# The last two units of attention values behind the next queries' transposes and scores

## Chip, core and metric

The kernel runs on one core of a Trainium2 chip. The metric is the device time of one execution in microseconds (us), as the median of several runs. The core has five engines with a queue each: TensorE (PE; its weight loads are shown as PEld), VectorE (DVE), ScalarE (ACT), GpSimd (POOL) and SyncE (SP). Each takes its instructions in the order of its queue, and the engines wait for one another by semaphores.

## What is computed

Two transformer blocks on x of shape (16, 256, 128) in float32. Each block is a layer norm and a mixture of experts (half weight), an attention, and a second mixture of experts. The first block's attention is causal with rotation and decay; the second one's has normed heads and no mask. Cut to what the change touches:

```python
# block 0, causal
scores = einsum('bhqd,bhkd->bhqk', q_rot, k_rot) / sqrt(8) + decay_bias   # 16 heads of 8
attn = softmax(where(causal, scores, -inf))
out = einsum('bhqk,bhkd->bhqd', attn, v)
x = x + reshape(out) @ Wo.T
# block 1, no mask
q, k, v = (layernorm_per_head(x @ W + b) for W, b in (...))
probs = softmax(einsum('bqhd,bkhd->bhqk', q, k) * 8 ** -0.5)
x = x + reshape(einsum('bhqk,bkhd->bqhd', probs, v)) @ Wo + bo
```

## The kernel before

The program is a row of stages: routing, experts, causal attention (`a0`), experts, routing, experts, second attention (`a1`), experts, and the last sum. Both attentions are one function, `attention_stage`, with a flag `causal`. It handles one batch of 256 tokens per step and keeps several batches in flight: in step s, TensorE makes the scores of batch s, the exponents' arguments and the values of batch s-1, the output of batch s-2, the routing of batch s-3, and the operands and projections of batches s+1 and s+2. `looped_steps` runs steps -3 to 18, the middle ones in a loop.

The order on each engine is written out by hand in its own `step`. A batch's attention is cut into 16 units of two heads and one half of the queries or keys. For a unit, TensorE makes raw scores (L1494) in one of two banks psS, VectorE takes their row maxima (L1066), and the maxima of all units, written into the query operand by `max_rows` (L1072, L1073), go through TensorE again: `queries` (L1513) transposes the query operand with its maxima, half t=0 into bank psA and half t=1 into psD. VectorE copies the first half to QM (L1080, `queries_out`), ScalarE the second (L1345). Then `e` (L1531, opened in the causal stage by a mask product, L1523) makes scores minus maxima, ScalarE takes the exponent into one of four buffers PT (L1362), and `unit_v` (L1555) multiplies by the values: two matmuls of 32 rows per unit into psV, for the units 8 to 15 into psV[1].

At the end of a step TensorE transposes the last operand (`operands`, L1473, n=3), does the values of units 14 and 15, and the next step begins with the queries of the batch whose maxima are done, the first two units' scores, the transposes of the routed rows (`routed_tiles`, L386) and the first exponent argument. The second half of the queries may not start before ScalarE has copied the operand n=2 out of psD (L1338, the copy a_KT<-a_psD).

VectorE closes a step with a row of jobs: `last_operand_out` (L1087), `queries_out` (L1080), `weighted_out` (L1093, which copies psV[1] of batch s-1 and waits for all 16 units of its values), `norm.dve_apply` of batch s+3 (L317, a_attn_out), `route.dve_norm` of batch s-2 (L314 and L317, a_route_out). The next step begins with the first unit's maximum (L1066). TensorE's routed transposes wait for a_route_out; its third unit of scores waits for the first unit's maximum; `back` (L1568) waits for `weighted_out`.

POOL has the scatter of routed rows, the reciprocal roots, in the causal stage the rotation, and in the second stage the scaling of heads (`scale_heads`, L961, L965, L969). The lines around the place are these:

```python
                if has(s + 1):
                    operands(s + 1, v, 3)
                if has(s - 1):
                    unit_v(s - 1, v, UNITS - 2)
                    unit_v(s - 1, v, UNITS - 1)
```

Of the kernel before, what the change touches and what calls it, by code (L numbers as in the profile page):

```python
# [662 lines left out]
def has(b, count=BATCHES):  # L663

    return not isinstance(b, int) or 0 <= b < count
# [113 lines left out]
def attention_stage(nc, keep, tag, slots_in, slots_out, causal, params, router, router_bias, capacity):  # L779
# [17 lines left out]
    with ExitStack() as ctx:  # L797
# [10 lines left out]
        UNITS = 16  # L808
# [98 lines left out]
        def unit_b(c):  # L907

            return c // 8, (c % 8) // 2, c % 2
# [509 lines left out]
        def _(pe):  # L1419
# [70 lines left out]
            def scores(u, c, hh):  # L1490
                t, g, r = unit_b(c)
                cols = P if causal and t == 0 else SEQ
                k = 2 * g + hh
                ins = nc.tensor.matmul(  # L1494
                    psS[c % 2][:, hh, 0:cols], QT[u][64 * r:64 * r + MAXR, k, t * P:(t + 1) * P],
                    KT[u][64 * r:64 * r + MAXR, k, 0:cols], start=not causal, stop=True, skip_group_check=True)
                if hh == 1:
                    ins.then_inc(s_S, 1)

            def queries(b, u, t):  # L1500
                if t == 0:
                    pe.wait_ge(s_m, b + 1)

                if has(b + 1):
                    pe.wait_ge(s_QK[1 + t], b + 2)
                elif t == 0:
                    pe.wait_ge(route.s_xnT, b - 2)
                else:
                    pe.wait_ge(route.norm.s_var, b - 1)
                src = ext[u][:, t, 0, :, :].rearrange("p h r -> p (h r)")  # L1510
                dst = (psA, psD)[t][:, :].bitcast(BF16)
                for k in range(8):
                    last = nc.tensor.transpose(dst[:, k * P:(k + 1) * P], src[:, k * P:(k + 1) * P], identb[:, :])  # L1513
                last.then_inc(s_Xm, 1)
# [91 lines left out]
            def step(s, u):  # L1606
                v = 1 - u
                if has(s - 1):
                    queries(s - 1, v, 0)
                    queries(s - 1, v, 1)  # L1610
                if has(s):
                    for c in range(2):
                        scores_open(s, c)
                    for hh in range(2):
                        for c in range(2):
                            scores(u, c, hh)
                if has(s - 3):
                    routed_tiles(s - 3, v)
                if has(s - 1):
                    e_open(s - 1, 0)  # L1620
                    for hh in range(2):
                        e(v, 0, hh)
                for n in range(UNITS):

                    if has(s) and n < UNITS - 2:
                        scores_open(s, n + 2)
                    if has(s - 1) and n < UNITS - 1:
                        e_open(s - 1, n + 1)
                    for hh in range(2):
                        if has(s) and n < UNITS - 2:  # L1630
                            scores(u, n + 2, hh)
                        if has(s - 1) and n < UNITS - 1:
                            e(v, n + 1, hh)

                    if has(s - 1) and n >= 2 and n % 2 == 0:
                        unit_v(s - 1, v, n - 2)
                        unit_v(s - 1, v, n - 1)
                    if n == 0 and has(s - 2):
                        back(s - 2, u, 0)
                    if n == 2 and has(s + 2):  # L1640
                        tiles(s + 2, u)
                    if n == 3 and has(s - 3):
                        logits(s - 3, v)
                    if n == 4 and has(s - 2):
                        back(s - 2, u, 1)
                    if n == 4 and has(s + 2):
                        project(s + 2, 0)
                    if n == 6 and has(s - 3):
                        route.pe_P(pe, s - 3, v, psD)
                    if n == 7 and has(s - 2):  # L1650
                        divided(s - 2)
                    if n == 7 and has(s + 2):
                        project(s + 2, 1)
                    if n == 10 and has(s - 2):
                        output(s - 2)
                    if n == 12 and has(s + 1):
                        operands(s + 1, v, 0)
                    if n == 13 and has(s + 1):
                        operands(s + 1, v, 1)
                    if n == 14 and has(s + 1):  # L1660
                        operands(s + 1, v, 2)
                if has(s + 1):
                    operands(s + 1, v, 3)
                if has(s - 1):
                    unit_v(s - 1, v, UNITS - 2)
                    unit_v(s - 1, v, UNITS - 1)

            looped_steps(pe, -3, 4, 12, 18, step)


# [381 lines left out]
```

## Time and profile before

| what | us |
|---|---|
| median of 3 runs | 1972.28 |
| lowest, highest | 1964.04, 1979.4 |
| profiled execution | 1987.22 |
| its span | 1985.4 |
| TensorE, VectorE, POOL, ScalarE busy | 1354.7, 1180.1, 938.6, 718.6 |

The profile is one execution; its times are counted from the start of its span. The causal attention runs from about 330 to 735, the second one from about 1240 to 1780. In a table of stretches, PEclk is the share of TensorE's full clock that was granted. In a row of the timeline the brackets name the idle time ahead of the first instruction and what ended it.

### The profile page before, as it was taken

What the parts mean: (1) busy time and instruction counts of PE and PEld (TensorE: products, weight loads), DVE (VectorE), ACT (ScalarE), POOL (GpSimd) and SP (SyncE); (2) the same over time, 40 slices, a digit from 0 to 9 for tenths busy, and PEclk for the clock granted to TensorE, in tenths of its full rate; (3) what the DMA queues carried; (4) which work ended last, traced back from release to release, by engine and by line L of the source; (5) the groups of instructions that cost most, each with busy time, mean ns of one, the idle gap of its engine ahead of it and who ended that gap; (6) DMA issues with size and microseconds to landing.
All of it is one profiled execution on the core that took longest, in us unless ns stands there. A gap on an engine that the chain in (4) does not pass through costs nothing. (4 is left out here: it accounts for less than half of the span.)

```text
span 1985.4 us, 34923 instructions
## 1 busy us (share of the span) xinstructions
PE 1354.7 (68%) x10592; PEld 870.5 (44%) x10592; DVE 1180.1 (59%) x4230; ACT 718.6 (36%) x1339; POOL 938.6 (47%) x1276
## 2 busy tenths in 40 slices
PE   1319955988889973992329944776777777856980
PEld 1208952444444433992218841333333333325870
DVE  3632226788887651225855536888777787743555
ACT  1102222766665531220003412554444545522330
POOL 2844543345444321554755745445454554333670
PEclk9999985999998896995559975786676677767995
DMA  6152220000000005222237840000000000015864
GB/s 227 45 116 61 73 64 16 12 23 26 22 16 12 12 17 115 72 69 76 72 81 213 245 137 16 11 12 12 16 16 16 16 6 12 8 33 159 236 199 130
DMA packets 93868, 134.91 MB, mean 68 GB/s; under 512 B 14784, under 2 KB 72512, under 8 KB 93760
## 3 DMA queue, kind: packets, MB, share of 16 engines
q1 hardware_dynamic: 62768, 88.27, 16.3%
q0 software_dynamic: 17408, 35.82, 5.3%
q10 hardware_dynamic: 13584, 9.48, 2.0%
q8 instruction: 56, 0.92, 0.2%
q14 instruction: 52, 0.43, 0.1%
HBM read 80.61 MB, written 52.91 MB: 67 GB/s over the span
## 5 line engine op out<-in xcount | busy, mean ns | idle before, releaser
L1362 ACT ACTIVATE a_PT<-a_psE 128x512 f32<-128x512 f32 (+1 forms) x512 | 275.5, 545 | 296.1 <-PE a_psE L1531 292.0
L1066 DVE TENSOR_REDUCE a_mx<-a_psS 128x2 f32<-128x512 f32 (+1 forms) x512 | 309.3, 617 | 22.6 <-PE a_psS L1494 21.9
L1494 PE MATMUL a_psS<-a_KT,a_QT 54*128 54x256 bf16 (+1 forms) x1024 | 206.0, 304 | 81.8 <-DVE a_mx L1066 69.4
L1531 PE MATMUL a_psE<-a_QM,a_KT 56*128 56x256 bf16 (+1 forms) x1024 | 209.0, 304 | 1.9 <-issue 0.8
L1555 PE MATMUL a_psV<-a_PT,a_vx 128*32 128x256 f32 (+1 forms) x2048 | 183.3, 436 | 0.0
L1946 POOL DMA_INDIRECT slots_y<-e_y,e_ids x160 | 155.3, 970 | 46.6 <-issue 24.4
L1876 PE MATMUL e_psH<-e_rowsT,e_w 128*128 128x256 f32 x640 | 162.6, 399 | 9.0 <-DMA e_w<-in_pack 7.6
L1494 PEld LDWEIGHTS a_psS<-a_KT,a_QT 54*128 54x128 bf16 x1024 | 60.7, 100 | 217.8 <-issue 119.0
L1793 POOL DMA_INDIRECT slots_y<-e_y,e_ids x128 | 124.2, 971 | 48.7 <-POOL e_ids L1791 29.2
L1876 PEld LDWEIGHTS e_psH<-e_rowsT,e_w 128*128 128x128 f32 x640 | 119.7, 197 | 28.1 <-issue 7.0
L1765 ACT ACTIVATE e_hT<-e_psH 128x1024 f32<-128x1024 f32 x64 | 65.5, 1023 | 183.0 <-PE e_psH L1738 183.0
L1738 PE MATMUL e_psH<-e_rowsT,kept_w 128*128 128x256 f32 x512 | 126.5, 392 | 2.1 <-DVE e_rowsT L1774 2.1
L1906 ACT ACTIVATE e_sg<-e_psH,e_w 128x256 f32<-128x256 f32 x160 | 67.1, 470 | 167.6 <-PE e_psH L1876 167.6
L1747 PE MATMUL e_psY<-kept_w,e_hT 128*128 128x128 f32 x1024 | 124.9, 276 | 0.0
L1747 PEld LDWEIGHTS e_psY<-kept_w,e_hT 128*128 128x128 f32 x1024 | 119.9, 193 | 0.1
L1774 DVE COPY e_rowsT<-e_psT 128x256 f32<-128x256 f32 x64 | 27.2, 425 | 146.9 <-PE e_psT L1730 146.9
L1915 DVE COPY e_rowsT<-e_psT 128x256 f32<-128x256 f32 x80 | 34.0, 425 | 129.7 <-PE e_psT L1869 129.7
L1738 PEld LDWEIGHTS e_psH<-e_rowsT,kept_w 128*128 128x128 f32 x512 | 95.7, 197 | 14.4 <-DVE e_rowsT L1774 3.5
L986 POOL TENSOR_TENSOR a_left<-a_left,a_ext 128x512 f32<-128x512 f32 x32 | 37.0, 1157 | 134.9 <-DVE a_ext L1055 134.9
L982 POOL TENSOR_TENSOR a_left<-a_qk,a_ext 128x512 f32<-128x512 f32 x32 | 37.0, 1157 | 112.0 <-DVE a_ext L1051 112.0
L522 POOL TENSOR_TENSOR a_rows<-a_rows,no_rows 128x4 int32<-128x4 int32 x32 | 6.3, 198 | 170.2 <-DVE a_rows L514 170.2
L1443 PE MATMUL a_psA<-a_wqkv,a_xaT 128*128 128x384 f32 x128 | 76.2, 688 | 15.3 <-DVE a_pr L1027 9.1
(328 smaller groups left out, 3189.1 us busy)
## 6 DMA issues: line engine op xcount, KB each, us to landing
e_w<-in_pack SPq DMA_DIRECT2D x80, 450.0 KB, 4.0
e_rows<-slots_x SPq DMA_DIRECT2D x80, 129.0 KB, 3.0
e_rows<-spans_x SPq DMA_DIRECT2D x64, 129.0 KB, 2.1
a_got<-slots_y SPq DMA_DIRECT2D x32, 256.0 KB
t_got<-slots_y SPq DMA_DIRECT2D x32, 256.0 KB, 2.9
slots_y<-e_y,e_ids POOLq DMA_INDIRECT x288, 2.2
spans_x<-tail ACTq DMA_DIRECT2D x8, 516.0 KB, 13.6
spans_x<-tail SPq DMA_DIRECT2D x8, 516.0 KB, 17.3
```

Of the source, the lines that this page charges most:

```text
L1066: nc.vector.tensor_reduce(mx[u][:, t, 4 * g + r:4 * g + r + 3:2], psS[c % 2][:, :, 0:cols], AX, ALU.max).then_inc(s_max, 1)
L1362: nc.scalar.activation(PT[:, c % 4, :, q0:SEQ], psE[c % 2][:, :, q0:SEQ], ACT.Exp).then_inc(s_e, 1)
L1443: nc.tensor.matmul(psA[:, 0:QKV], xaT[:, t * P:(t + 1) * P], wqkv[:, :], start=True, stop=True).then_inc(s_proj, 1)
L1494: ins = nc.tensor.matmul(psS[c % 2][:, hh, 0:cols], QT[u][64 * r:64 * r + MAXR, k, t * P:(t + 1) * P], KT[u][64 * r:64 * r + MAXR, k, 0:co ...
L1531: ins = nc.tensor.matmul(psE[c % 2][:, hh, q0:SEQ], KT[u][64 * r:64 * r + MAXR + 2, k, kt * P:(kt + 1) * P], QM[64 * r:64 * r + MAXR + 2, ...
L1555: last = nc.tensor.matmul(psV[g // 2][32 * quad:32 * quad + 32, g % 2, q0:SEQ], vx[u][:, kt, head, :], PT[:, c % 4, hh, q0:SEQ], start=(kt ...
L1738: last = nc.tensor.matmul(psH[j % 2][:, c, :], w[:, j // KEPT_TILES, c * P:(c + 1) * P], rowsT[:, j % 2, :], start=True, stop=True)
L1747: last = nc.tensor.matmul(psY[j % 2][:, s * D:(s + 1) * D], hT[:, j % 2, c, s * P:(s + 1) * P], w[:, j // KEPT_TILES, UP + c * D:UP + (c + ...
L1793: pool.indirect_dma_start(slots_out, bass.IndirectOffsetOnAxis(ap=ids[:, j % U, s:s + 1].bitcast(U32), axis=0), y[:, j % U, s, :], None).t ...
L1876: last = nc.tensor.matmul(psH[u % 2][:, c, :], w[:, u, c * P:(c + 1) * P], rowsT[:, u % 2, :], start=True, stop=True)
L1906: ins = nc.scalar.activation(sg[:, u % 2, c, :], psH[u % 2][:, c, :], ACT.Silu, bias=w[:, u, B1 + c:B1 + c + 1])
L1946: pool.indirect_dma_start(slots_out, bass.IndirectOffsetOnAxis(ap=ids[:, u, s:s + 1].bitcast(U32), axis=0), y[:, u, s, :], None).then_inc( ...
```

## The change

The values of units 14 and 15 leave the end of the step. In the next step they stand behind the queries (both halves) and the scores of the first two units, and ahead of the routed transposes. The batch is then numbered s-2, and its buffers have the index u.

```diff
@@ -1614,6 +1614,9 @@
                     for hh in range(2):
                         for c in range(2):
                             scores(u, c, hh)
+                if has(s - 2):
+                    unit_v(s - 2, u, UNITS - 2)
+                    unit_v(s - 2, u, UNITS - 1)
                 if has(s - 3):
                     routed_tiles(s - 3, v)
                 if has(s - 1):
@@ -1661,9 +1664,6 @@
                         operands(s + 1, v, 2)
                 if has(s + 1):
                     operands(s + 1, v, 3)
-                if has(s - 1):
-                    unit_v(s - 1, v, UNITS - 2)
-                    unit_v(s - 1, v, UNITS - 1)
 
             looped_steps(pe, -3, 4, 12, 18, step)
```

On TensorE, at a step's boundary in the causal stage (`a_psV<-a_PT` are the values, `a_psA` and `a_psD<-a_identb` the two halves of the queries, `a_psS` the masks and scores):

```order
 L1473 MATMUL a_psD<-a_identb,a_ext 128x128 x8
 L1473 MATMUL a_psV<-a_identb,a_ext 128x128 x8
-L1555 MATMUL a_psV<-a_PT,a_vx 32x128 x4
 L1513 MATMUL a_psA<-a_identb,a_ext 128x128 x8
 L1513 MATMUL a_psD<-a_identb,a_ext 128x128 x8
 L1486 MATMUL a_psS<-a_masks,a_identb 128x2x128 x2
 L1494 MATMUL a_psS<-a_KT,a_QT 128x128 x4
+L1555 MATMUL a_psV<-a_PT,a_vx 32x128 x4
 L386 MATMUL a_psA<-ident,a_route_out 128x128 x2
 L1523 MATMUL a_psE<-a_masks,a_identb 128x2x128
```

Four matmuls pass 16 transposes, two masks and four score products; nothing else changes place.

The same place in the second attention stage, where the values have 256 columns and there are no masks:

```order
 L1473 MATMUL a_psD<-a_identb,a_ext 128x128 x8
 L1473 MATMUL a_psV<-a_identb,a_ext 128x128 x8
-L1555 MATMUL a_psV<-a_PT,a_vx 32x256 x4
 L1513 MATMUL a_psA<-a_identb,a_ext 128x128 x8
 L1513 MATMUL a_psD<-a_identb,a_ext 128x128 x8
 L1494 MATMUL a_psS<-a_KT,a_QT 128x256 x4
+L1555 MATMUL a_psV<-a_PT,a_vx 32x256 x4
 L386 MATMUL a_psA<-ident,a_route_out 128x128 x2
 L1531 MATMUL a_psE<-a_QM,a_KT 128x256 x2
```

Here too the values stand ahead of the routed transposes and the first exponent argument.

VectorE's queue is the same in both kernels. Its row from the copy of the weighted values (L1093) over the loop's end to the first maximum of the next step (L1066):

```order
L1093 COPY a_oT<-a_psV 128x512
L169 REGISTER_ALU
L317 TENSOR_SCALAR a_attn_out<-x_res,a_attn_mv,a_attn_rstd 128x128 x2
L314 ISA
L314 COPY a_route_out<-ids 128x4
L317 TENSOR_SCALAR a_route_out<-x_res,a_route_mv,a_route_rstd 128x2x128 x2
L194 ISA
L652 REGISTER_ALU
L652 COMPARE_AND_BRANCH
L1066 TENSOR_REDUCE a_mx<-a_psS 128x2
```

Nothing moved in it; its first row waits for the matmuls that moved on TensorE.

## Rows read from the trace of the kernel before

**Rows 1.** The page, its first part: busy time, share and instructions.

```profile
PE 1354.7 (68%) x10592; PEld 870.5 (44%) x10592; DVE 1180.1 (59%) x4230; ACT 718.6 (36%) x1339; POOL 938.6 (47%) x1276
```

**Rows 2.** Stretches: length, busy PE, PEld, DVE, ACT, POOL; PEclk; DMA share; GB/s.

```profile
391.33:581.88 190.55, 170.34 (x1916) 89.22 (x1914) 162.91 (x569) 125.62 (x264) 95.58 (x119) 1.00 0.07 23
581.88:691.58 109.70, 100.20 (x954) 48.62 (x952) 75.28 (x260) 62.49 (x129) 44.15 (x54) 0.81 0.03 11
1339.98:1691.61 351.63, 259.27 (x2074) 120.12 (x2075) 269.21 (x759) 170.86 (x320) 174.00 (x253) 0.71 0.04 13
...
611.90:625.50 13.60, 13.60 (x80) 6.03 (x82) 6.95 (x32) 6.36 (x16) 2.31 (x2) 0.50 0.01 1
```

**Rows 3.** Timeline of TensorE: start, length, engine, line, operation, count, idle before.

```profile
607.58 0.42 PE L1555 MATMUL a_psV<-a_PT,a_vx 128*32 128x128 f32 x8
607.93 0.62 PE L1513 MATMUL a_psA<-a_identb,a_ext 128*128 128x128 bf16 x8
608.39 0.61 PE L1513 MATMUL a_psD<-a_identb,a_ext 128*128 128x128 bf16 x8
608.84 0.38 PE L1486 MATMUL a_psS<-a_masks,a_identb 128*128 128x256 bf16 x2
609.15 0.28 PE L1494 MATMUL a_psS<-a_KT,a_QT 54*128 54x128 bf16 x4
611.25 0.41 PE L386 MATMUL a_psA<-ident,a_route_out 128*128 128x128 f32 x2 [1.82 <-DVE a_route_out L317]
```

**Rows 4.** Timeline of ScalarE, the same boundary.

```profile
607.31 1.01 ACT L1338 COPY a_KT<-a_psD 128x1024 bf16<-128x1024 bf16 x1
609.04 1.01 ACT L1345 COPY a_QM<-a_psD 128x1024 bf16<-128x1024 bf16 x1 [0.71 <-PE a_psD L1513]
```

**Rows 5.** Timeline of VectorE, the same boundary.

```profile
607.68 0.69 DVE L1087 COPY a_KT<-a_psV 128x512 uint32<-128x512 uint32 x1 [0.38 <-PE a_psV L1473]
608.59 0.69 DVE L1080 COPY a_QM<-a_psA 128x512 uint32<-128x512 uint32 x1 [0.22 <-PE a_psA L1513]
609.20 0.68 DVE L1093 COPY a_oT<-a_psV 128x512 f32<-128x512 f32 x1
609.80 0.59 DVE L317 TENSOR_SCALAR a_attn_out<-x_res,a_attn_mv,a_attn_rstd 128x128 f32 x2
...
610.37 0.73 DVE L317 TENSOR_SCALAR a_route_out<-x_res,a_route_mv,a_route_rstd 128x256 f32 x2
611.02 0.42 DVE L1066 TENSOR_REDUCE a_mx<-a_psS 128x2 f32<-128x256 f32 x1
```

**Rows 6.** Waits from 390 to 694: us in total, times, longest.

```profile
PE a_psA L386 <- DVE a_route_out L317: 22.8, 13, 1.9
```

**Rows 7.** Groups by line and shape (busy us, mean ns): 390 to 694, 1340 to 1692.

```profile
L317 DVE TENSOR_SCALAR a_attn_out<-x_res,a_attn_mv,a_attn_rstd 128x128 f32 x16 | 4.8, 339 | 0.0
...
L317 DVE TENSOR_SCALAR a_attn_out<-x_res,a_attn_mv,a_attn_rstd 128x128 f32 x16 | 17.2, 1117 | 0.0
```

**Rows 8.** Timeline of VectorE at a boundary of the second stage.

```profile
1341.19 0.59 DVE L317 TENSOR_SCALAR a_attn_out<-x_res,a_attn_mv,a_attn_rstd 128x128 f32<-128x128 f32 x2
...
1341.77 2.11 DVE L317 TENSOR_SCALAR a_route_out<-x_res,a_route_mv,a_route_rstd 128x256 f32<-128x256 f32 x2
...
1347.17 0.68 DVE L1066 TENSOR_REDUCE a_mx<-a_psS 128x2 f32<-128x512 f32 x1
```

**Rows 9.** Timeline of POOL, the boundary of rows 8.

```profile
1342.21 1.52 POOL L961 TENSOR_TENSOR a_pt<-a_pr,a_hv 128x768 f32<-128x768 f32 x1
...
1345.84 1.26 POOL L969 TENSOR_TENSOR a_qk<-a_pt,a_par 128x512 f32<-128x512 f32 x1 [0.23 <-POOL a_pt L965]
```

**Rows 10.** Timeline of VectorE at another boundary of the second stage.

```profile
1413.49 3.01 DVE L317 TENSOR_SCALAR a_attn_out<-x_res,a_attn_mv,a_attn_rstd 128x128 f32 x2
...
1416.50 1.67 DVE L317 TENSOR_SCALAR a_route_out<-x_res,a_route_mv,a_route_rstd 128x256 f32 x2
```

**Rows 11.** Timeline of POOL, the boundary of rows 10.

```profile
1414.63 1.80 POOL L965 TENSOR_TENSOR a_pt<-a_pt,a_par 128x768 f32<-128x768 f32 x1
```

## The prediction

> **What bounds the kernel now.** I read the page's engine line first [rows 1]: no engine fills the span, TensorE with 68% comes nearest, so stages are limited by chains between engines. The edit touches only the two attention stages, and there only the boundary between two steps, so the next view is a table of stretches [rows 2]. Eight steps of the causal stage take 190.55 us, 23.82 each, with TensorE granted its full clock (PEclk 1.00); the next four take 109.70, 27.4 each, at 0.81. Ten steps of the second attention stage take 351.63, 35.2 each, at 0.71. Inside the four slow ones lies a stretch of 13.6 us at 0.50, the 1.2 GHz level. A step's length therefore hangs on what is in it and on the clock.
>
> Then one boundary on three engines, the one at 608.59, where VectorE starts copying the first half of the shifted queries. TensorE [rows 3] issues the batch's last values (four matmuls, each shown as two, 607.58), eight query transposes (607.93), eight more (608.39), two masks and four score matmuls (608.84 to 609.43), and then stands still until 611.25, 1.82 us, for the routed rows. ScalarE [rows 4] copies an operand from 607.31 to 608.32; the second query transposes wait for this copy, since they write the bank that it reads, and start just behind it. VectorE [rows 5] copies the first query half at 608.59, the weighted values (L1093) at 609.20, then makes two normalised tiles (609.80), the routed rows (610.37 to 611.10), and only then reads the first maximum (611.02). What sets the restart is thus VectorE's row of five jobs, not TensorE and not the exps. The waits view confirms it over the causal stage: TensorE waited 13 times for route_out, 22.8 us together [rows 6].
>
> **The change part by part.** No instruction is added or taken away: four value matmuls go from ahead of the queries to behind the scores at each boundary. VectorE's and ScalarE's orders stay.
>
> What goes at the front: the four matmuls hold the queue from 607.58 to 607.93, 0.35 us [rows 3]. The first transposes can start that much earlier; their maxima have been ready for longer. The second transposes can't: they stand at 608.39 because of ScalarE's copy that ends at 608.32 [rows 4]. So the second query half, the scores and ScalarE's L1345 stay in place, and the gain at the front is 0. VectorE's query copy may start about 0.2 earlier (its own copy before it, 607.68 plus 0.69, ends at 608.37 [rows 5]), which buys nothing, because its next job now waits for the values.
>
> What is late next: L1093 waits for all of a batch's values. They begin behind the last score, whose end is 609.43; four of them took 0.42 us from first start to last end [rows 3]. That gives 609.43 + 0.42 = 609.85 in place of 609.20: 0.65 us later. Bounds: 0.5 if they overlap the last score, 1.1 if they run at the half clock (both scores and values about twice as long). Queued behind L1093 are the norm tiles, the routed rows and the first maximum, without a gap between them [rows 5], and TensorE's routed transposes, the first exp product and the third score product wait for those. All move by 0.65. For the causal stage that is 13 x 0.65 = 8.5 us. I take nothing off: from this point each unit's scores wait for maxima and each product for exps, and both begin later.
>
> Second stage. Here a step also has POOL's head scaling (three instructions, L961, L965, L969). At 1341.19 VectorE did two tiles in 0.59 us; the routed rows behind them took 2.11 and ended at 1343.88 [rows 8], just after L961 had ended (1342.21 + 1.52 = 1343.73), and the second maximum came only at 1347.17, behind the end of L969 (1345.84 + 1.26 = 1347.10) [rows 9]. At 1413.49 the same two tiles took 3.01 us and ended at 1416.50 [rows 10], just behind L965 (1414.63 + 1.80 = 1416.43) [rows 11], and the routed rows then took 1.67 more. Grouped, such a tile took 1117 ns here and 339 in the causal stage [rows 7]. So a norm instruction that meets POOL's scaling waits until that ends, and gets through between two of them. I went through the ten boundaries of this stretch, of which rows 8 and rows 10 are the two kinds. Where VectorE already waits (7 of 10), L1093 coming 0.2 to 0.85 later is hidden: 0. In the other three (rows 8 is the first) four value matmuls of 256 columns I put 0.2 longer than the causal ones (twice the columns), which makes 0.65 + 0.2 = 0.85; the tiles begin at about 1341.19 + 0.85 = 1342.04, and only one is through before L961 starts. The other waits until 1343.8, the routed rows until L965 or L969 ends. TensorE then gets them 2.2 to 3.4 later, the second maximum about 1.3 later. Lower bound 0 (POOL lets them through), upper 3.4; I take 1.5, near the maximum that paces the scores: 3 x 1.5 = 4.5 us. The boundary at 1717.68 has no scaling: 0.8. The last boundary of each stage has no scores; there the values follow the queries and nothing moves.
>
> By the Trainium skill (SBUF — State Buffer, "SBUF: two separate sides"), VectorE and GpSimd hold a shared pair of ports in turn, whoever starts first, and the other fully blocks. Applied to every POOL instruction it would also hold the causal tiles behind the rotation, and starting later would give about 0.1 to 0.2 back at each of 13 boundaries, 2 us less in the sum. The trace doesn't show that: in the causal stage those tiles took 339 ns [rows 7], the pair of 609.80 no more than 0.59 together [rows 5]. I leave it out.
>
> The clock. The four slow steps in [rows 2] are the causal boundaries after 581.88; at the second of them the granted clock is 0.50 from 611.90 on, behind TensorE's 1.8 us of idleness, though the eight steps before had the same one. So it is near the point where it falls. The change lengthens that idleness to about 611.90 - 609.80 = 2.1 us and opens a gap of about 0.35 ahead of the second transposes. Steps become 24.5 long, so the place of the boundary against the clock's own changes wanders, where it had stood still for eight steps. I count seven of 13 boundaries with a fall in place of four. A fall costs 27.4 - 23.8 = 3.6 us [rows 2]: 3 x 3.6 = 10.8 us, with 0 and 9 x 3.6 = 32 as its ends. The second stage has fallen clocks nearly everywhere; 0 there.
>
> The Trainium skill (TensorE: Matmul & The Clock Gate, "What's actually happening") says the ramp penalty is under 1% of a typical kernel's span and needs no model. By that rule the sum would stop 10.8 lower. The trace has four such steps costing 14.5 us, 0.7% of the span, in this one stage, so I keep the term.
>
> Sum: 8.5 + 0.8 + 4.5 + 10.8 = 24.6 us on the profiled execution's 1987.2 (its span is 1985.4), which lies 14.9 above the median of the runs. Nothing in the terms depends on that offset, so I set them on the median: 1972.3 + 24.6 = 1996.9 us.
>
> **The rivals.**
> Only the wait of VectorE shows, ports and clock stay as they are: 8.5 + 0.8 = 9.3, 1981.6 us. For it: the runs of before spread over 15 us, more than these terms. Against it: the longer idleness.
> The clock falls at every causal boundary: 13.8 + 32 = 46, 2018 us. For it: a step with a fall, 27.4, may put the next boundary at the same place again, as it did four times running. Against it: the first eight.
> Not slower: the moved matmuls fill part of the idle time, and the clock holds. From the point where the idleness ends up shorter than 1.8 us, all four falls go: 9.3 - 14.4 = -5, 1967 us. For it: the values now run within the stretch that had been idle. Against it: what ends the idleness waits for them, so it moves along.
> Also not slower: the transposes gain at the front. If the second ones were free at once, 0.35 at some 26 boundaries would go, 9 us, 1963. Against it: 608.32 and 608.39.
>
> **How the numbers follow.** Forecast 0.45, only the wait 0.23, clock at every boundary 0.15, clock holds 0.11, gain at the front 0.06. About 1% (19.7 us of 1972.3) is what a measurement of this kernel tells from no change: slower means above 1992. Of the forecast 0.31 lies above it, of the third case all 0.15, of the second 0.04: slower 0.50. Faster, below 1952.6, needs the fourth case with much of the second stage's slow clock gone too: 0.04. The rest, 0.46, is within 1%. The range leaves out the fourth and fifth and a part of the third: 1974 to 2019.
>
> **What would show it.** Right: in the causal stage L1093 starts about 0.65 later against the end of ScalarE's operand copy (609.20 - 608.32 = 0.88 now, 1.5 then), TensorE's wait for the routed rows starts later and ends 0.65 later, full-clock steps are 24.5; the norm tiles of some boundaries of the second stage take 1.5 to 2 us where they took 0.59. Wrong: full-clock causal steps of 23.8 or less; a boundary where the second transposes start before the operand copy ends; or fewer stretches at the half clock.

## The result and the profile after

| | before | after |
|---|---|---|
| median us | 1975.47 (1964.04 to 1979.4, 4 runs) | 2012.05 (2005.9 to 2018.17, 4 runs) |
| span of the profiled execution | 1985.4 | 2004.1 |

The ratio is 1.0203, with an interval of 1.0164 to 1.0241: the change makes the kernel 2% slower. In a second comparison (e10), on a chip where the kernel before takes 2029.3 us, it was 1.0149 (1.0115 to 1.0182). A ratio compares the faster executions of each kernel alone, while the medians and ranges given for the kernel before are of all its executions. The medians lie 36.6 us apart and the profiled spans only 18.7: the profiled execution of the kernel before (1987.22) lies above its four runs, that of the changed kernel (2005.9) is the fastest of its four.

The page's engine line of the changed kernel, which answers to [rows 1]:

```profile
PE 1356.6 (68%) x10592; PEld 874.9 (44%) x10592; DVE 1173.1 (59%) x4230; ACT 719.7 (36%) x1339; POOL 938.7 (47%) x1276
```

The counts are the same, and TensorE is busy 1.9 us more while the span is 18.7 longer. So the time is not in work, and the stretches must tell where it is. The table of stretches of the changed kernel (length, busy PE, PEld, DVE, ACT, POOL, then PEclk, DMA share and GB/s), to be read against [rows 2]:

```profile
417.54:442.06 24.52, 21.40 (x239) 11.29 (x239) 20.34 (x73) 15.70 (x34) 12.26 (x16) 1.00 0.08 23
468.00:685.86 217.86, 193.06 (x1912) 96.23 (x1912) 157.39 (x558) 127.09 (x265) 95.74 (x120) 0.87 0.05 16
498.50:505.30 6.80, 6.48 (x37) 2.79 (x38) 4.35 (x15) 2.52 (x6) 1.16 (x1) 0.50 0.00 0
525.80:532.60 6.80, 6.54 (x37) 2.83 (x38) 4.28 (x15) 2.52 (x6) 1.15 (x1) 0.50 0.00 0
```

One causal step with the whole clock takes 24.52 us in place of 23.82. The eight steps from 468.00 to 685.86 take 27.23 each, at 0.87, and the two short rows show why: a stretch of 6.8 us at 0.50, the 1.2 GHz level, then the next one 27.3 us later, and so on. One fall per step, each beginning 3.2 to 3.6 us behind the query copy and in the last half microsecond of TensorE's idle stretch (498.50, where the routed transposes start at 498.82). The kernel before had four stretches at half clock in this stage, 41.0 us in all; this one has twelve, 88.7 us, in twelve of its 13 steps from 391.7 on.

A boundary of the causal stage in the changed kernel. TensorE's timeline, which answers to [rows 3]:

```profile
416.86 0.62 PE L1513 MATMUL a_psA<-a_identb,a_ext 128*128 128x128 bf16 x8
417.62 0.62 PE L1513 MATMUL a_psD<-a_identb,a_ext 128*128 128x128 bf16 x8
418.08 0.38 PE L1486 MATMUL a_psS<-a_masks,a_identb 128*128 128x256 bf16 x2
418.39 0.29 PE L1494 MATMUL a_psS<-a_KT,a_QT 54*128 54x128 bf16 x4
418.61 0.43 PE L1555 MATMUL a_psV<-a_PT,a_vx 128*32 128x128 f32 x8
421.20 0.41 PE L386 MATMUL a_psA<-ident,a_route_out 128*128 128x128 f32 x2 [2.16 <-DVE a_route_out L317]
```

ScalarE's operand copy there, which answers to [rows 4]:

```profile
416.54 1.03 ACT L1338 COPY a_KT<-a_psD 128x1024 bf16<-128x1024 bf16 x1
```

VectorE, which answers to [rows 5]:

```profile
417.54 0.68 DVE L1080 COPY a_QM<-a_psA 128x512 uint32<-128x512 uint32 x1
419.13 0.69 DVE L1093 COPY a_oT<-a_psV 128x512 f32<-128x512 f32 x1 [0.91 <-PE a_psV L1555]
419.74 0.59 DVE L317 TENSOR_SCALAR a_attn_out<-x_res,a_attn_mv,a_attn_rstd 128x128 f32<-128x128 f32 x2
420.25 0.16 DVE L314 COPY a_route_out<-ids 128x4 int32<-128x4 int32 x1
420.32 0.73 DVE L317 TENSOR_SCALAR a_route_out<-x_res,a_route_mv,a_route_rstd 128x256 f32<-128x256 f32 x2
420.96 0.41 DVE L1066 TENSOR_REDUCE a_mx<-a_psS 128x2 f32<-128x256 f32 x1
```

The common point of both kernels is the end of ScalarE's copy, 608.32 before and 417.57 here. L1093 starts 0.88 us behind it before and 1.56 here; the bracket names what it waited for, the values. The routed transposes start 2.93 behind it before and 3.63 here. TensorE stands still for 2.16 us where it had been 1.82.

### The profile page after: what moved, and what is told of

Same layout as the page of the kernel before. It is cut to its first block and busy times, and to the rows that moved or that the text cites. A ratio compares the mean times of both kernels' runs of the same rounds, so it can differ in the third digit from the quotient of the medians.

```text
span 2004.1 us, 34923 instructions
## 1 busy us (share of the span) xinstructions
PE 1356.6 (68%) x10592; PEld 874.9 (44%) x10592; DVE 1173.1 (59%) x4230; ACT 719.7 (36%) x1339; POOL 938.7 (47%) x1276
## 5 line engine op out<-in xcount | busy, mean ns | idle before, releaser
L1066 DVE TENSOR_REDUCE a_mx<-a_psS 128x2 f32<-128x512 f32 (+1 forms) x512 | 309.0, 616 | 32.1 <-PE a_psS L1494 30.9
L1494 PE MATMUL a_psS<-a_KT,a_QT 54*128 54x256 bf16 (+1 forms) x1024 | 201.8, 300 | 82.8 <-DVE a_mx L1066 71.2
L1555 PE MATMUL a_psV<-a_PT,a_vx 128*32 128x256 f32 (+1 forms) x2048 | 177.0, 423 | 0.0
L1774 DVE COPY e_rowsT<-e_psT 128x256 f32<-128x256 f32 x64 | 27.1, 424 | 146.9 <-PE e_psT L1730 146.9
L386 PE MATMUL a_psA<-ident,a_route_out 128*128 128x128 f32 x64 | 18.4, 384 | 104.1 <-DVE a_route_out L317 104.1
## 6 DMA issues: line engine op xcount, KB each, us to landing
spans_x<-tail SPq DMA_DIRECT2D x8, 516.0 KB, 16.6
```

Source lines behind the costliest of these rows:

```text
L1066: nc.vector.tensor_reduce(mx[u][:, t, 4 * g + r:4 * g + r + 3:2], psS[c % 2][:, :, 0:cols], AX, ALU.max).then_inc(s_max, 1)
L1494: ins = nc.tensor.matmul(psS[c % 2][:, hh, 0:cols], QT[u][64 * r:64 * r + MAXR, k, t * P:(t + 1) * P], KT[u][64 * r:64 * r + MAXR, k, 0:co ...
L1555: last = nc.tensor.matmul(psV[g // 2][32 * quad:32 * quad + 32, g % 2, q0:SEQ], vx[u][:, kt, head, :], PT[:, c % 4, hh, q0:SEQ], start=(kt ...
```

## The experiments

To compare the stages I took, from each trace, the time from the first to the sixteenth query copy (L1080 on VectorE), "causal", and from the seventeenth to the last, "second". In order of the table: the ratio to the kernel before, and of the profiled execution, in us, these two lengths and the time at half clock within the causal one.

| kernel | ratio, interval | causal | second | causal, at half clock |
|---|---|---|---|---|
| before | 1 | 362.8 | 491.1 | 41.0 |
| after | 1.0203 (1.0164 to 1.0241) | 391.7 | 481.6 | 88.7 |
| e1: after, L1093 behind the norm tiles | 0.9882 (0.9836 to 0.9928) | 348.5 | 491.6 | 0 |
| e2: before, L1093 behind the norm tiles | 1.0026 (0.9985 to 1.0066) | 374.6 | 489.3 | 68.3 |
| e3: after, filler | 1.0003 (0.9965 to 1.0041) | 357.7 | 490.6 | 3.4 |
| e4: change in the causal stage alone | 1.0137 (1.0086 to 1.0189) | 395.5 | 489.8 | 99.0 |
| e5: before, filler | 0.9901 (0.9866 to 0.9936) | 347.5 | 494.7 | 0 |
| e6: values ahead of the scores | 1.0007 (0.9964 to 1.005) | not read | not read | not read |
| e7: before, norm tiles late | 0.9962 (0.9911 to 1.0013) | 350.7 | 492.5 | 3.4 |
| e8: after, norm tiles late | 0.9826 (0.9792 to 0.9859) | 349.9 | 482.0 | 0 |
| e9: change in the second stage alone | 1.0024 (0.9997 to 1.0051) | 374.1 | 497.8 | 34.1 |
| e10: after, again | 1.0149 (1.0115 to 1.0182) | 397.8 | 489.7 | 54.6 |
| e11: after, norm tiles behind the third maximum | 0.9914 (0.9879 to 0.9948) | 360.1 | 479.6 | 5.1 |
| e12: e8 with the change in the second stage alone | 0.9954 (0.9918 to 0.999) | 354.0 | 484.3 | 13.7 |

e1 to e4 ran on one chip and e5 to e8 on the same; e9 to e11 on another, where the kernel before took 2029.3 us (median) in place of 1979.5 to 1986.2; e12 on a third. The kernel before itself ranges over 1951 to 2010 us even without the slower chip, so I compare ratios, and stages only where they differ by more than a few us. What lies outside the two stretches takes 1113.5 to 1132.5 us in the traces of before, after and e1 to e8, so two spans can also differ by up to 19 us there.

### e3 and e5: is it the clock, or the wait?

In both, twelve matmuls of no use fill a part of TensorE's idle stretch (e3: the changed kernel, e5: the kernel before):

```diff
+                if has(s - 3):
+                    for _ in range(12):
+                        nc.tensor.matmul(psE[1][:, :, 0:P], identb[:, :],
+                                         identb[:, :].unsqueeze(1).to_broadcast([P, 2, P]), start=True, stop=True,
+                                         skip_group_check=True)
                 if has(s - 3):
                     routed_tiles(s - 3, v)
```

Expected of e3:

> The changed kernel, with 12 matmuls of no use (identity times identity, 256 columns, into the exponent bank that is rewritten later) ahead of the routed transposes: about 1.3 us of work at the full clock inside the idle stretch. They change no result. Theory (the clock falls because of the idle stretch, and that fall is most of the cost): the causal stage keeps its clock, steps 24.5 instead of 27.3, about 28 us come back there, and the second stage gains too if its clock holds better: 1950 to 1985. Rival (the cost is the wait alone, the clock falls for other reasons): no gain, or a loss of up to 1.3 us a boundary where the matmuls run at the half clock, 2010 to 2030.

Expected of e5:

> The kernel before, with the 12 matmuls of e3 at the same place. With the clock held in both, e3 minus this one is the wait alone, without the clock. Theory (the wait moves the first maximum by 0.7 us and the step follows it): causal steps of 23.8 at the full clock against 24.5 in e3, some 9 us in the causal stage; time 1955 to 1968, about 0.5% under e3. Rival (a held clock hides the wait, or the filler's benefit is of another kind): no difference to e3 beyond 3 us in the causal stage.

Measured: 1971.8 us for e3, 1962.1 for e5. TensorE's timeline of e3 at a causal boundary shows the filler in the gap:

```profile
415.24 0.42 PE L1555 MATMUL a_psV<-a_PT,a_vx 128*32 128x128 f32 x8
415.60 1.48 PE L1622 MATMUL a_psE<-a_identb 128*128 128x256 bf16 x12
417.82 0.41 PE L386 MATMUL a_psA<-ident,a_route_out 128*128 128x128 f32 x2 [0.74 <-DVE a_route_out L317]
```

Eight causal steps of e3, as a stretch:

```profile
389.79:585.74 195.95, 182.25 (x2008) 98.01 (x2008) 162.79 (x570) 125.70 (x265) 95.85 (x119) 1.00 0.07 22
```

The same eight steps of e5:

```profile
389.89:580.37 190.48, 181.63 (x2012) 97.93 (x2010) 162.77 (x569) 125.63 (x264) 95.63 (x119) 1.00 0.07 23
```

Both of these stretches are at the whole clock throughout, and the filler itself costs a step nothing: 24.49 and 23.81 us, against 24.52 and 23.82 in the whole-clock steps without it. So the wait alone costs 0.68 to 0.70 per boundary, and 357.7 - 347.5 = 10.2 us in the causal stage. Up to 1.2 of the 10.2 may be clock: e3 has one stretch of 3.4 us at half clock, at 370.3, and that step is 1.9 us longer than e5's instead of 0.7. The filler computes nothing anyone reads; it took 34.0 us off the causal stage of the changed kernel (391.7 to 357.7) and 15.3 off the one before (362.8 to 347.5). This settles it for that stage, for these traces: of the 28.9 us by which it grew, 9.0 to 10.2 are wait and the rest, 34.0 - 15.3 = 18.7 or up to 19.9, is clock. TensorE was busy for more of the stage and the stage became shorter; the rival (no gain, or a loss) is refuted. The gain in the second stage that I had thought possible is not there: with the filler that stage is 3.6 us (e5) and 9.0 us (e3) longer in the traces, and the same changed kernel gives 481.6 and 489.7 in two traces (after, e10), so this says neither loss nor gain.

What e3 shows is that filling the idle stretch keeps the clock up. It does not show that the falls came from the stretch being longer; e2, below, speaks against its length as the whole cause.

### e4 and e9: which stage?

e4 is the change under `causal`, e9 under `not causal`, with the old two lines kept for the other:

```diff
-                if has(s - 2):
+                if has(s - 2) and causal:
                     unit_v(s - 2, u, UNITS - 2)
                     unit_v(s - 2, u, UNITS - 1)
...
+                if has(s - 1) and not causal:
+                    unit_v(s - 1, v, UNITS - 2)
+                    unit_v(s - 1, v, UNITS - 1)
```

Expected of e4:

> The change made in the causal stage alone; the second attention keeps the old order. Theory: the cost sits in the causal stage (its part of the trace grew by 29 us, the second stage's shrank by 8), so the whole of it stays: 2003 to 2017, 1.5 to 2.1% over the kernel before. Rival (the second stage's three instructions of POOL take a good part): 1985 to 1998.

Expected of e9:

> The change made in the second attention alone; the causal stage keeps the old order. Theory (the cost is the causal stage's, 10 us of wait and the rest clock; in the second stage POOL's scaling sets when the norm tiles are done, whatever the values do): within 0.4% of the kernel before. Rival (the forecast's term: three boundaries later by 1.5 us or more): 5 to 12 us slower, 0.3 to 0.6%.

Measured: e4 2006.4 us, as expected, 1.4% over the kernel before, with a causal stage of 395.5. Its trace repeats the pattern of the changed kernel: ten steps running of 27.1 to 27.3 us, a fall in each. e9 is at 1.0024, an interval that holds both no difference and the 5 us of the rival. The causal stage carries the cost; whether the second one adds up to 0.5% was not separated from nothing.

### e1 and e2: who waits behind L1093?

On VectorE, in both (e1: the changed kernel, e2: the kernel before):

```diff
-                if has(s - 1):
-                    weighted_out(s - 1, v)
                 if has(s + 3):
                     norm.dve_apply(dve, s + 3, v)
                 if has(s - 2):
                     route.dve_norm(dve, s - 2, u, u)
+                if has(s - 1):
+                    weighted_out(s - 1, v)
```

Expected of e1:

> The changed kernel, with VectorE's copy of the weighted values (L1093) moved behind the norm tiles and the routed rows, so that these no longer stand behind the wait for the moved values. Theory (the cost comes through VectorE's row: what is queued behind L1093 waits, TensorE idles longer, and its clock falls): the routed transposes come about 1.9 us earlier against ScalarE's operand copy (3.6 now), the idle stretch ahead of them shrinks under 1 us, the clock stays up in the causal stage, its steps fall from 27.3 to about 23.2, and the time comes to 1960 or less, under the kernel before. Rival (the cost lies in TensorE's order itself, four matmuls between the scores and the exponent arguments): only 0.4 us a boundary comes back, the time stays above 1995.

Expected of e2:

> The kernel before, with the same move of L1093 on VectorE alone. Theory: the routed rows come 0.6 us earlier, idle time 1.2 instead of 1.8 us, no fallen clock in the causal stage, full-clock steps 23.2 to 23.8: 1945 to 1970 us. If the queue behind L1093 doesn't matter, the time is that of the kernel before within 0.5%. Set beside e1 it tells what the move of the values is worth once nobody waits behind them: theory 0 to 0.3 us a boundary faster with the move.

Measured: e1 1955.6 us, below the kernel before, which holds for the theory against its rival. The routed transposes came 1.0 us earlier and not 1.9, the idle stretch is 1.16 us and not under 1. e2 is level with the kernel before (1988.9, ratio 1.0026), where it was to be under 1970. In both, the steps were not the 23.2 that I expected: causal steps of e1 take 24.1, all at the whole clock. This stretch of e1 is seven of them:

```profile
435.51:604.19 168.68, 151.27 (x1673) 78.05 (x1673) 145.94 (x498) 109.97 (x232) 84.57 (x106) 1.00 0.07 21
```

e2's causal stage should have had no fallen clock. It has eight stretches, 68.3 us at half clock where the kernel before has 41.0, and steps that alternate between 29.4 and 25.3 us. TensorE's routed transposes at one of its boundaries, and the half-clock stretch behind them:

```profile
523.26 0.44 PE L386 MATMUL a_psA<-ident,a_route_out 128*128 128x128 f32 x2 [1.69 <-DVE a_route_out L317]
523.90:537.50 13.60, 13.60 (x80) 6.03 (x82) 7.94 (x34) 6.29 (x16) 2.31 (x2) 0.50 0.06 19
```

At the fourth to tenth boundary of the stage the idle stretch is 1.60 to 1.78 us in e2 and 1.73 to 1.86 in the kernel before. Shortly after each of these seven the clock falls in e2, and after none of them in the kernel before. So between the 1.16 us of e1 (no fall) and the 2.16 of the changed kernel (a fall in nearly every step) the length of this stretch does not say whether the clock falls; what does stays open.

Set side by side, e1 and e2 differ by the move of the values alone: e1 is 33.3 us faster by the medians, and its causal stage 26.1 us shorter. With the copy out of the way the moved values fill part of the idle stretch (1.16 us left, where e2 has 1.69 or 1.78) and e1 keeps its clock; without a fall the two have steps of like length (the last ones, 23.8 and 23.5 against 24.0 and 23.5). That is the fourth case of my prediction (the moved matmuls fill idle time and the clock holds), once nobody waits behind the values.

e2's timeline of VectorE at a boundary tells what I had missed of the steps:

```profile
520.73 0.69 DVE L1080 COPY a_QM<-a_psA 128x512 uint32<-128x512 uint32 x1 [0.22 <-PE a_psA L1513]
521.33 1.15 DVE L317 TENSOR_SCALAR a_attn_out<-x_res,a_attn_mv,a_attn_rstd 128x128 f32 x2
522.41 0.16 DVE L314 COPY a_route_out<-ids 128x4 int32 x1
522.48 0.72 DVE L317 TENSOR_SCALAR a_route_out<-x_res,a_route_mv,a_route_rstd 128x256 f32 x2
523.12 0.68 DVE L1093 COPY a_oT<-a_psV 128x512 f32<-128x512 f32 x1
523.73 0.41 DVE L1066 TENSOR_REDUCE a_mx<-a_psS 128x2 f32<-128x256 f32 x1
```

And POOL's, at the same boundary:

```profile
520.73 0.73 POOL L942 TENSOR_TENSOR a_qk<-a_pt 128x256 f32<-128x256 f32 x1
521.42 0.72 POOL L943 TENSOR_TENSOR a_qk<-a_pt 128x256 f32<-128x256 f32 x1
```

The two tiles take 1.15 us instead of 0.59 and end 0.34 behind the end of POOL's rotation (522.14), which is one tile's length. So in the causal stage too a norm tile waits for a POOL instruction in flight, and L1093, which reads PSUM and had stood ahead of the tiles, had filled just that time. Moved earlier, the tiles wait where the copy had worked, and the copy comes on top: the first maximum is 0.6 us later than before, measured from ScalarE's copy.

How early VectorE gets to its maxima sets the step. The fourth maximum starts 6.26 us behind the end of ScalarE's copy in the kernel before, 6.55 in e1 and 6.96 in e3, and a step with the whole clock is 17.5 to 17.6 us longer than that in all three.

### e6: the values between queries and scores

```diff
+                if has(s - 2):
+                    unit_v(s - 2, u, UNITS - 2)
+                    unit_v(s - 2, u, UNITS - 1)
                 if has(s):
                     for c in range(2):
                         scores_open(s, c)
                     for hh in range(2):
                         for c in range(2):
                             scores(u, c, hh)
-                if has(s - 2):
-                    unit_v(s - 2, u, UNITS - 2)
-                    unit_v(s - 2, u, UNITS - 1)
```

> The values stand behind both halves of the queries but ahead of the first scores. Theory: L1093 waits for the values alone, about 0.25 to 0.35 less than in the changed kernel (two masks and four scores fewer ahead of them), the scores come 0.35 later but VectorE is not ready for the first maximum anyway; full-clock steps 24.1 to 24.3 against 24.5 and 23.8, idle stretch near 2.3 us, so the clock falls at most causal boundaries still: 1995 to 2012. Rival (the place behind the scores itself is what costs): back to the time of the kernel before, 1985 or less.

Measured: 1974.1 us, ratio 1.0007, where 1995 or more was expected. That is the rival's time. Its profiled execution is the slowest of its thirteen (2006.9 us), so I read no stage from it. One thing in it doesn't depend on that: L1093 starts 1.13 us behind ScalarE's copy, against 0.88 before and 1.56 in the changed kernel: 0.43 less, a little more than the theory wanted, and 0.25 more than before. My estimate of the idle stretch was wrong: the scores now end behind the values and cover part of it, so it is 1.6 us, less than the 1.82 of before. So most of the cost is gone when the values stand ahead of the scores; how much of that is wait and how much is clock, no trace tells.

### e7 and e8: VectorE's row taken apart

e7 is the kernel before and e8 the changed one; on VectorE only the routed rows stay at the step's end:

```diff
-                if has(s - 1):
-                    weighted_out(s - 1, v)
-                if has(s + 3):
-                    norm.dve_apply(dve, s + 3, v)
                 if has(s - 2):
                     route.dve_norm(dve, s - 2, u, u)
...
                 maxima(0, 1)
+                if has(s - 2):
+                    weighted_out(s - 2, u)
+                maxima(1, 2)
+                if has(s + 2):
+                    norm.dve_apply(dve, s + 2, u)
                 if has(s + 3):
                     comb.dve_gate(dve, link, s + 3, v)
                 add(0, 0)
-                maxima(1, 2)
```

Expected of e7:

> The kernel before on TensorE; on VectorE only the routed rows stay at the step's end, the copy L1093 comes behind the first maximum of the next step and the norm tiles behind the second. Theory (a causal step follows the first maximum, which e1 and e2 moved by +0.3 and +0.6 with steps of 24.1 and about 24.4): the first maximum comes 0.6 us or more earlier, the idle stretch shrinks under 1.5 us, full-clock steps 23.0 to 23.4, clock held: 1935 to 1960. Rival (the step follows the routed transposes): the same gain only if those come earlier, which POOL's rotation can prevent: 1965 to 1990.

Expected of e8:

> The changed kernel with VectorE's order of e7. Nobody waits behind the moved values but L1093 itself, which now stands behind the first maximum. Theory: the move costs nothing any more, within 0.5% of e7, 1935 to 1960. Rival (the move costs by its place in TensorE's queue, ahead of the routed transposes and the first exponent arguments): over 10 us slower than e7.

Measured: e7 1965.0 us, e8 1948.4. With nobody queued behind the moved values, the change costs nothing; it is 16.6 us faster than the old order. Both expectations missed on a side: the causal steps are 24.3 and not 23.4, since the third maximum comes 4.9 us behind ScalarE's copy (4.4 before, 5.1 after). The same jobs stand ahead of it as before, in another order. What is added is a wait for POOL: the routed rows now start 1.1 us earlier, while the rotation still runs (it ends 1.7 us behind the copy), and take 1.22 us in place of 0.73, which is the 0.49 that the third maximum and all later ones lose. And "within 0.5%" was too narrow: the causal stages are level (350.7 and 349.9), the second is 10.5 us shorter in e8, and 5.6 of the 16.9 us between the two spans lie in neither. VectorE's timeline of e7 in that stage:

```profile
1401.49 0.16 DVE L314 COPY a_route_out<-ids 128x4 int32 x1
1401.56 3.60 DVE L317 TENSOR_SCALAR a_route_out<-x_res,a_route_mv,a_route_rstd 128x256 f32 x2
```

POOL's, there:

```profile
1401.61 1.52 POOL L961 TENSOR_TENSOR a_pt<-a_pr,a_hv 128x768 f32<-128x768 f32 x1
1403.21 1.80 POOL L965 TENSOR_TENSOR a_pt<-a_pt,a_par 128x768 f32<-128x768 f32 x1
```

VectorE's of e8, at a boundary of the same stage:

```profile
1394.01 0.80 DVE L317 TENSOR_SCALAR a_route_out<-x_res,a_route_mv,a_route_rstd 128x256 f32 x2
```

POOL's of e8, there:

```profile
1394.74 1.52 POOL L961 TENSOR_TENSOR a_pt<-a_pr,a_hv 128x768 f32<-128x768 f32 x1
```

In e7 the routed rows begin with POOL's scaling and take 3.60 us; in e8 they are through in 0.80, before it starts. Of ten boundaries, counted from the fourth of the stage, e8 has six at which they take 1.04 us or less, and e7 has one. That fits the moved values: the query copy ahead of the routed rows no longer stands behind them. e8's second stage also has 41 us less at half clock (237.6 against 278.5), and no run tells how much of the 10.5 us is due to either.

### e12: is the gain of e8 the second stage's?

The edit is e8's on VectorE with e9's on TensorE.

> VectorE's order of e7 and e8, with the values moved in the second attention alone. e8 was 16.6 us under e7; in the traces the causal stages are equal (349.9 and 350.7) and the second stage of e8 is 10.5 shorter. Theory (in the second stage the query copy comes earlier once the values are gone from ahead of it, and the routed rows get past VectorE before POOL's scaling starts): the ratio to the kernel before is that of e8, 0.983, within 0.5 points, and the second stage takes 480 to 485 us. Rival (the gain was spread over executions, not the second stage's): the ratio is e7's, 0.996, and the second stage takes 489 or more.

Measured: the second stage took 484.3 us, as the theory wanted; the ratio, 0.9954, is the rival's. Its median, 1957.2, lies between e8's and e7's, but on another chip; set against the medians of the kernel before measured beside them, e8, e12 and e7 are at 0.984, 0.987 and 0.993. Its causal stage has a fallen clock in it (one step of 27.6 among steps of 24.3). So the second stage's gain is seen in the trace, and the whole of e8's lead over e7 is not explained by it.

### e10 and e11

Expected of e10:

> The changed kernel as it is, in more rounds and with a second profile, beside e9 on one chip. Theory: the causal steps are again 27.2 to 27.3 us with a fallen clock in nearly each, 1.5 to 2.2% over the kernel before. If the pattern of steps was an accident of one execution, the second profile shows steps of 24.5 in a good part and times spread over 30 us.

The second profile has causal steps of 27.0 to 30.4 us for eleven steps running, each with a fall: the pattern is no accident. It is not the same one, though: nine of these falls last 3.4 us and two 10.2, and the stage has 54.6 us at half clock, not 88.7. Steps without a fall are longer on this chip too (24.8 in e9, not 23.8), so their lengths can't be set beside those of the first trace. Its time, 2055.9, is 1.5% over the kernel before on that chip.

e11 is the changed kernel on TensorE; on VectorE it takes L1093 and the norm tiles out of the step's end as e7 does, and puts the tiles behind the third maximum:

```diff
                 maxima(0, 1)
+                if has(s - 2):
+                    weighted_out(s - 2, u)
...
                 maxima(2, 3)
+                if has(s + 2):
+                    norm.dve_apply(dve, s + 2, u)
                 add(0, 1)
```

> The changed kernel on TensorE; on VectorE the routed rows at the step's end, L1093 behind the first maximum, the norm tiles behind the third one. Theory (a causal step follows the third maximum, 4.4 us after ScalarE's operand copy before, 5.1 with the change, 4.9 in e7 and e8): it comes at 4.3 or less, causal steps 23.8 or less at the full clock, 6 us or more under e8 if the second stage stays: 1935 to 1950. Rival (the number of jobs ahead of the later maxima counts, not their place): steps 24.3 again, e8's time within 0.3%.

Measured: 0.9914, 2009.5 us on the slower chip. The third maximum came 3.5 us behind ScalarE's copy, 1.4 earlier than in e8, as wanted, but the steps are 24.8 to 25.0 and not 23.8. VectorE and POOL behind the third maximum (520.70):

```profile
521.03 1.32 DVE L317 TENSOR_SCALAR a_attn_out<-x_res,a_attn_mv,a_attn_rstd 128x128 f32 x2
```

```profile
520.87 1.16 POOL L982 TENSOR_TENSOR a_left<-a_qk,a_ext 128x512 f32<-128x512 f32 x1 [3.46 <-DVE a_ext L1051]
```

The tiles meet another instruction of POOL there and take 1.32 us instead of 0.59. The fourth maximum comes 5.86 us behind ScalarE's copy. e9, on the same chip and with the old causal order, has its third one at 3.99, its fourth at 5.87, and steps of 24.84 where the clock is whole, against 24.79 in e11. So the gain at the third maximum was gone by the fourth, and the step followed the fourth. Against e8 the maxima from the fourth to the fourteenth are 0.9 earlier; then up to 1.6 us went at one point, where TensorE's transposes of an operand paused 0.28 us with no releaser shown. e9 has the same loss there (its fifteenth maximum is 2.15 us behind the fourteenth, 0.61 in e8), so it was not e11's own. By its ratio e11 is behind e8 (0.9826), against the theory and the rival both; which is faster on one chip stays open.

## Why the prediction was right or wrong

The direction was right and the time, 2012.05, lies in the range; the size was too small, 24.6 us forecast against 36.6 between the medians. That the time lies in the range owes something to luck: the range reached that far only for a part of the third case (a fall at every boundary, 2018), 15 us above the forecast, and in the traces the terms miss in opposite directions, the causal stage 28.9 us longer where 19.3 were forecast, the second 9.5 shorter where 5.3 longer were. Step by step:

**The front gains nothing.** Right in the causal stage: the second query transposes start 0.05 us behind ScalarE's copy, where it was 0.07, though the first now start 0.76 ahead of them instead of 0.46.

**The wait at L1093, 0.65 us by 13.** Right: 0.68 by the timeline, 0.70 by the steps of e3 and e5, 9.0 to 10.2 us against 8.5. It passes through the whole step: between e5 and e3 every maximum and every exp of a step is 0.7 later.

**The second stage, 5.3 us.** The mechanism is there and its price is not. VectorE's timeline of the changed kernel at a boundary where POOL's scaling starts late:

```profile
1542.14 0.69 DVE L1093 COPY a_oT<-a_psV 128x512 f32<-128x512 f32 x1 [1.10 <-PE a_psV L1555]
1542.75 3.55 DVE L317 TENSOR_SCALAR a_attn_out<-x_res,a_attn_mv,a_attn_rstd 128x128 f32 x2
...
1546.29 1.79 DVE L317 TENSOR_SCALAR a_route_out<-x_res,a_route_mv,a_route_rstd 128x256 f32 x2
```

The tiles that took 0.59 in [rows 8] take 3.55, and the routed rows end 3.6 us later, measured from ScalarE's copy. The step that follows takes 36.06 us, and that of [rows 8] took 35.96, but with 16.4 us at half clock against 20.5, so the two can't be set against each other. Two steps of this kind with the same 23.9 us at half clock took 38.11 (after, at 1366) and 37.67 (before, at 1484), 0.4 apart, where I had put 1.5. As a whole the second stage was shorter in the changed kernel's trace (481.6 against 491.1, with 215 us at half clock against 266), and 489.7 in e10's. e9 puts the term at 0.24% with an interval from nothing to 0.5%; my 5.3 us is 0.27%, so its size is neither confirmed nor refuted.

**The clock, 10.8 us.** This is the mis-sized term: 18.7 us. That the falls hang on the idle stretch is what e3 shows, by filling it. That they came because it grew to 2.16 us is not shown: e2's is no longer than before, and its clock falls more often. What failed is the step on where the falls go: I let the place "wander" and counted seven of 13 boundaries, where twelve have one. A step with a fall in it took 27.23 us, the next fall came 27.3 us on, at nearly the same place of the next step, and so for eight steps in a row. That is the picture of my third case, to which I gave 0.15; that the step's length sets the place is how I read it, and no run varied it by itself. A fall cost 2.7 us (27.23 - 24.52) and not 3.6. The 3.6 had been read rightly from the kernel before, whose falls last longer: by the filler, its four cost 15.3 us and the twelve of the changed kernel 34.0, which is 0.37 and 0.38 us for each microsecond at half clock.

**The rule on the clock that I had not followed.** Measured, the half clock cost the causal stage of the changed kernel 34.0 us, 1.7% of its span. The prediction had kept the term against the Trainium skill's rule (TensorE: Matmul & The Clock Gate, "What's actually happening") that the ramp penalty is under 1% of a typical span. That rule speaks of a typical kernel; in this one falls recur with the steps, and keeping the term was right.

**The ports.** I left the wait for the rotation out, since the pair of tiles took its usual 0.59 us in [rows 5]. For the sum that was right: from the start of L1093 to the end of the routed rows it is 1.9 us in both kernels, so nothing was given back. As a statement on the causal stage it was wrong. e2 shows the wait, 1.15 us for the pair, and e7 and e11 show it too; the first tile of [rows 5] had begun only 0.2 us ahead of the rotation's end (1.7 us behind ScalarE's copy there too). This agrees with the exclusive lock of the Trainium skill (SBUF — State Buffer, "SBUF: two separate sides"), which I had doubted for the rotation.

In the profiled executions the causal stage is 28.9 us longer, the second 9.5 shorter and the rest 0.7 shorter: 18.7 us. Only the causal part is explained by experiments. The 36.6 us between the medians can't be split in the same way; the other 8 lie within what the kernel before varies by.

## What to carry to other kernels

Work that is moved past others takes its consumer's wait with it: look at what stands behind the consumer on its engine, and move that too, for the same move cost 2.0% with the old row on VectorE, gained 33.3 us when one job of that row had changed place (e1 against e2), and 16.6 us when the row had been taken apart (e8 against e7). A wait that moves has two prices here, its length and the time at half clock that comes with it, and the second was the larger. If steps are alike, a fall can repeat with the steps: in every one (after, e4, e10), in every second one (e9), or in one alone (e12). So give the term a wide range, read its price from steps at either clock, and try a few useless matmuls in the wait.

The version to keep is e8: 1948.4 us, 1.7% under the kernel before on the same chip (its six runs took 1944.6 to 1952.7 us, 18 of the kernel before 1952.0 to 1999.2), with the changed order on TensorE and the norm tiles out of VectorE's last row.

## What the runs showed that I had not expected

Useless matmuls in a wait made the unchanged kernel faster by 1.0% (e5). The kernel before ranges from 1951 to 2010 us on two of the chips; e1, e5 and e8, whose causal stages hold the whole clock in the trace, range over 8 to 11 us in six runs each, so a good part of that spread is probably the clock's, which I did not test by itself. The granted clock of the runs points the same way: of 23 runs of the kernel before on one chip the fastest, 1951.3 us, had 0.826 and the slowest, 2007.3, had 0.795. A causal step follows the fourth maximum and not the routed transposes: in e7 and e8 those came 0.6 to 0.7 us earlier than before and the step was 0.5 longer. On the chip of e1 to e8 the third maximum would serve as well, and I had taken it for the pace; e11 tells the two apart.
